# A two-graph attention network on one core: the edges' load, the masks' order, one buffer layout and the third border are changed

## The reference, cut to what matters

```python
e     = leaky_relu(s_src[src] + s_dst[dst], 0.2)      # one score per edge and head
emax  = segment_max(e, dst)
alpha = exp(e - emax[dst]) / segment_sum(exp(e - emax[dst]), dst)
out   = segment_sum(alpha[:, :, None] * h[src], dst) + bias
...
x = layernorm(x + gnn0(x, edges)); x = layernorm(x + gnn1(x, edges, types))
```

## Time and profile before

| | us |
|---|---|
| median of three runs | 1907.76 (1905.82 to 1907.84) |
| profiled execution, its own time | 1906.95 |
| its span, first to last instruction | 1905.1 |
| PE busy | 1777.2 (93%) |
| DVE busy | 1549.3 (81%) |
| ACT busy | 727.1 (38%) |

### The profile page before, as it was taken

How to read it: one execution, slowest core, us unless ns; L and a number is a source line. 1 busy time by engine, 2 the same in 40 slices (tenths; PEclk the granted TensorE clock), 3 DMA queues, 4 the chain that set the end, 5 groups by cost and what they waited for, 6 DMA issues and landing times.

```text
span 1905.1 us, 24263 instructions
## 1 busy us (share of the span) xinstructions
PE 1777.2 (93%) x8426; PEld 1337.9 (70%) x8427; DVE 1549.3 (81%) x2949; ACT 727.1 (38%) x1248; POOL 21.6 (1%) x40
## 2 busy tenths in 40 slices
PE   4889977699999899999999999998999999999997
PEld 3544545599754455555899999997899975555554
DVE  7898878899568555999999999996556648998996
ACT  4898976443124221111444444442311222332331
POOL 0000011010000000000000000000000000000000
PEclk8999998799999899999999999998999999999999
DMA  6200169351350326766412122121266467767764
GB/s 184 68 23 22 59 216 359 119 158 31 115 171 17 148 87 222 261 219 193 145 57 87 59 70 75 57 60 33 81 214 208 148 223 272 247 222 249 252 214 165
DMA packets 168068, 276.66 MB, mean 145 GB/s; under 512 B 11819, under 2 KB 132386, under 8 KB 164486
## 3 DMA queue, kind: packets, MB, share of 16 engines
q1 hardware_dynamic: 115942, 212.43, 34.4%
q10 hardware_dynamic: 48736, 48.48, 7.9%
q0 software_dynamic: 3264, 14.16, 2.1%
HBM read 219.31 MB, written 55.71 MB: 144 GB/s over the span
## 4 chain that ended last, share of the span: by engine, by line
PE 79%; DVE 12%; issue 3%; DMA 2%; ACT 2%; DVEq 1%; ACTq 0%; SPq 0%
PE ps L1406 26%; PE ps L1435 17%; PE ps L1359 12%; PE ps L1266 9%; PE ps L1064 3%; PE ps L1081 3%; PE ps L1169 2%; DVE work L1982 2%; PE ps L1198 2%; PE ps L1317 2%; DVE feat L2063 1%; DVE work L2394 1%; PE ps L1151 1%; DVE work L2388 1%; DVE feat L2359 1%
## 5 line engine op out<-in xcount | busy, mean ns | idle before, releaser
L1435 PE MATMUL ps<-work 128*128 128x384 f32 (+1 forms) x784 | 256.5, 486 | 2.0 <-DVE work L2149 2.0
L1359 PE MATMUL ps<-work 128*128 128x384 f32 (+1 forms) x720 | 237.9, 491 | 3.2 <-ACT work L1726 2.6
L1406 PE MATMUL ps<-counts,work 128*128 128x193 f32 x1440 | 239.3, 327 | 0.0
L1406 PEld LDWEIGHTS ps<-counts,work 128*128 128x128 f32 x1440 | 235.9, 190 | 0.3 <-DVE work L2394 0.3
L1820 ACT ACTIVATE work<-work,s 128x1280 f32<-128x1280 f32 x111 | 151.3, 1363 | 213.8 <-DVE work L2388 211.6
L1435 PEld LDWEIGHTS ps<-work 128*128 128x128 f32 x784 | 148.4, 189 | 107.1 <-DVE work L2149 2.6
L1359 PEld LDWEIGHTS ps<-work 128*128 128x128 f32 x720 | 136.9, 191 | 101.2 <-issue 16.3
L2394 DVE SCALAR_TENSOR_TENSOR work<-work,counts 128x1280 f32<-128x1280 f32 x112 | 166.3, 1485 | 2.0 <-SPq L569 2.0
L1406 PE MATMUL ps<-counts 128*128 128x193 f32 x960 | 160.9, 327 | 1.1 <-ACTq L569 1.1
L1982 DVE TENSOR_SCALAR work<-work,winoff 125x480 bf16<-125x480 f16 x480 | 158.4, 399 | 0.6 <-issue 0.5
L1406 PEld LDWEIGHTS ps<-counts 128*128 128x128 f32 x960 | 157.4, 190 | 1.7 <-ACTq L569 1.7
(11 more groups left out here) (295 smaller groups left out, 2597.8 us busy)
## 6 DMA issues: line engine op xcount, KB each, us to landing
work<-hs_d SPq DMA_DIRECT2D x75, 960.0 KB, 5.3
work<-nomask_d SPq DMA_DIRECT2D x70, 320.0 KB, 3.1
work<-pqrow_d SPq DMA_DIRECT2D x12, 1280.0 KB, 6.4
nomask_d<-work SPq DMA_DIRECT2D x40, 320.0 KB, 7.3
hx_d<-work ACTq DMA_DIRECT2D x60, 192.0 KB, 2.4
counts<-hx_d SPq DMA_DIRECT2D x120, 96.0 KB, 1.9
hs_d<-feat ACTq DMA_DIRECT2D x22, 480.0 KB, 3.6
counts<-pqrow_d SPq DMA_DIRECT2D x6, 1280.0 KB, 6.0
```

The costliest lines, as they stand in the source:

```text
L1359: last = mm(bank(n % 4 if i else n % 2, cols), xT[:, j, t * P:(t + 1) * P], wv[:, j, :], start=(j == 0), stop=(j == DT - 1))
L1406: last = mm(sums_at(c, t, u), xe_of(c)[i % RING][:, t * P:(t + 1) * P], hx[:, i % RING, 0:1 + c.width], start=(r == 0 and k == 0 and t % T ...
L1435: last = mm(bank(product_bank(g, i), width), a[:, at * P:(at + 1) * P], h_block(n, block_, width), start=(m == 0), stop=(m == STEPS_D - 1) ...
```

## The change

- SP waits for the edges before it issues `cols`, `wt_b`, `rhs` and `x`; ACT waits for the edges before it issues `wt_a`.
- The window bounds are computed for three chunks at once by six instructions; most of the edges' keys are made while PE turns the bounds; `bnd_ready` 3 lets ACT and PE read the table before `keys_ready`; ACT runs one small `Abs` early.
- Masks: the total mask of tile t+1 comes ahead of the type masks of tile t, and DVE alternates one mask and one search.
- `hx_a` moves from the masks' region to the front of `work`, with the `xe_a` buffers behind it. SP loads the features ahead of the last three masks' stores, DVE waits only until all masks are turned, and the first `weights` come ahead of the border.
- `keep_clock`: 24 transposes of the identity at the end of layer B, and 24, 24 and 16 around the first pieces of layer C.
- Before layer D ACT copies the turned tiles 0 and 1 each one `elu_exp` earlier.

```diff
-        hx_a = carve(work, (RING + 4) * NP, RING * H2C).rearrange("p (s c) -> p s c", s=RING)
+        hx_a = carve(work, 4 * NP, RING * H2C).rearrange("p (s c) -> p s c", s=RING)
-        xe_a = [carve(work, (4 + i) * NP, NP) for i in range(RING)]
+        xe_a = [carve(work, 4 * NP + RING * H2C + i * NP, NP) for i in range(RING)]
-        MASKS = [(TOTAL, 0)] + [(r if r < RELS else TOTAL, t if r < RELS else t + 1) for t in range(T) for r in range(RELS + 1)]
+        MASKS = [(TOTAL, 0)] + [m for t in range(T) for m in [*[(TOTAL, t + 1)] * (t + 1 < T), *((r, t) for r in range(RELS))]]
...
+            sp.wait_ge(e_in, 16 * 3)
             sp.dma_start(cols[:, :], t_in["cols"]).then_inc(cols_in, 16)
...
                     sp.dma_start(pqb_a[0], pqrow_d[0:2, :].partition_broadcast(P)).then_inc(s.pq_in[0].sem, 16)
+                    sp.wait_ge(v_done, len(WT_HALVES))
+                    for i in range(3):
+                        sp.wait_ge(*s.hx_out[i].at(16 * ring_share(2 * T, i, 3)))
+                    for k in range(RING):
+                        sp.dma_start(hx_a[:, k, 1:1 + HA], ga_d[k * P:(k + 1) * P, 0:HA]).then_inc(s.hx_in[k].sem, 16)
...
+            def keep_clock(n, at):
+                for _ in range(n):
+                    nc.tensor.transpose(ps[:, at:at + P // 2].bitcast(BF16), identb[:, :], identb[:, :])
...
+            pe.wait_ge(bnd_ready, 3)
+            extras = pe.value_load(tab[0:1, NW:NW + 1], min_val=0, max_val=MAXG)
             pe.wait_ge(keys_ready, 1)
-            extras = pe.value_load(tab[0:1, NW:NW + 1], min_val=0, max_val=MAXG)
...
                     b_attention(s)
+                    pe.wait_ge(o2_copied, 1)
+                    keep_clock(24, 2 * 512)
                     end_phase(pe, ph)
...
                     second_layer(0)
+                    keep_clock(24, 512)
                     second_layer(1)
+                    keep_clock(24, 512)
                     turn(0)
+                    keep_clock(16, 512)
...
-            act.wait_ge(s_chunkin, 32)
+            act.wait_ge(e_in, 16 * 3)
...
+            nc.scalar.activation(mm_[0:1, 0, 0:1], epsc[0:1, :], ACT.Abs)
+            act.wait_ge(bnd_ready, 3)
...
-                for e in range(3):
+                for e in range(2):
                     elu_exp(e)
-                fetch_turned(0)
-                elu_exp(3)
-                fetch_turned(1)
+                for e in range(2):
+                    fetch_turned(e)
+                    elu_exp(e + 2)
...
-            for a in range(3):
-                link(v.tensor_scalar(tmp_w, iota_w, cmin[:, a:a + 1], None, ALU.is_ge))
-                link(v.scalar_tensor_tensor(tmp_w, iota_w, cmax[:, a:a + 1], tmp_w, ALU.is_le, ALU.mult))
-                v.tensor_scalar(act_w[:, 0, a, :], tmp_w, cidm[:, a:a + 1], 1000.0, ALU.mult, ALU.add)
-                link(v.tensor_scalar(act_w[:, 1, a, :], tmp_w, cidp[:, a:a + 1], None, ALU.mult))
+            v.tensor_tensor(from_w, windows, by_chunk(cmin), ALU.is_ge)
+            link(v.tensor_tensor(upto_w, windows, by_chunk(cmax), ALU.is_le))
+            link(v.tensor_tensor(from_w, from_w, upto_w, ALU.mult))
+            link(v.tensor_tensor(act_w[:, 0, :, :], from_w, by_chunk(cidm), ALU.mult))
+            v.tensor_tensor(act_w[:, 1, :, :], from_w, by_chunk(cidp), ALU.mult)
+            link(v.tensor_scalar(act_w[:, 0, :, :], act_w[:, 0, :, :], 1000.0, None, ALU.add))
             v.nop().then_inc(bnd_ready, 1)
+            dve.wait_ge(e_in, 16 * 3)
+            ...   (five of the keys' instructions, two more behind bnd_ready 2, one behind bnd_ready 3)
             dve.wait_ge(bnd_turned, 1)
...
+                for t in range(T - 1):
+                    no_edges(4 * t + 1)
+                    dve.wait_ge(nm_copied, max(4 * t - 2, 1))
+                    if t == 0:
+                        dve.wait_ge(*s.s_in[0].at(16))
+                    search_a(t, 0)
+                    no_edges(4 * t + 2)
+                    search_a(t, 1)
+                    no_edges(4 * t + 3)
+                    if t == LAG:
+                        dve.wait_ge(*s.s_in[1].at(16))
+                    if t >= LAG:
+                        search_a(t - LAG, 2)
+                    no_edges(4 * t + 4)
+                    if t >= LAG:
+                        search_a(t - LAG, 3)
...
                 if c is A:
                     dve.wait_ge(v_turned, len(WT_HALVES))
+                    dve.wait_ge(nm_turned, 4 * T)
                     for i in range(2):
                         exponents(i, i, i, 0, 0, 16, 0, NP)
-                    for i in range(MASKS_OUT):
-                        dve.wait_ge(*nm_out_s[i].at(16 * ring_share(RELS * T, i, MASKS_OUT)))
                     v.memset(hx_a[:, :, 0:1], 1.0).then_inc(ones, 1)
+                    weights(0, 0, 0, c.rels[0], 0, NP)
```

More of the change, by code:

```diff
@@ L276, in gnn_program @@
         oh_hi = [take(WROW // 2, BF16) for _ in range(OH * WCH + 1)]
-        after_slots, space[0] = space[0], 16648 - 3272
+        after_slots, space[0] = space[0], 16648 - 3672
         src_i, dst_i, typ_i, win_i, tile_i = (take(NCH, I32) for _ in range(5))
@@ L281, in gnn_program @@
         cmin, cmax, cid, cidm, cidp = (take(4)[:, 0:3] for _ in range(5))
-        iota_w, tmp_w = take(NW), take(NW)
+        iota_w = take(NW)
+        from_w, upto_w = (take(3 * NW).rearrange("p (a w) -> p a w", a=3) for _ in range(2))
         act_w = take(6 * NW).rearrange("p (s a w) -> p s a w", s=2, a=3)
@@ L665, in _ @@
                 sp.wait_ge(*nm_out_s[i].at(16 * ring_share(RELS * T, i, MASKS_OUT)))
-            for i in range(3):
-                sp.wait_ge(*s.hx_out[i].at(16 * ring_share(2 * T, i, 3)))
-            for k in range(RING):
-                sp.dma_start(hx_a[:, k, 1:1 + HA], ga_d[k * P:(k + 1) * P, 0:HA]).then_inc(s.hx_in[k].sem, 16)
             for landed in total_out:
@@ L1531, in _ @@
             extras = act.value_load(tab[0:1, NW:NW + 1], min_val=0, max_val=MAXG)
+            act.wait_ge(keys_ready, 1)
             with act.If(extras < 1):
@@ L1934, in _ @@
             v.nop().then_inc(bnd_ready, 1)
+            v.scalar_tensor_tensor(keyf[0:EC, :], tile_i[0:EC, :], float(W), keyf[0:EC, :], ALU.mult, ALU.add)
+            v.scalar_tensor_tensor(lof[0:EC, :], tile_i[0:EC, :], -float(P), src_i[0:EC, :], ALU.mult, ALU.add)
             dve.wait_ge(bnd_turned, 2)
@@ L2068, in searches_a @@
                 no_edges(0)
-                for t in range(T + LAG - 1):
-                    masks = range(4 * t + 1, min(4 * t + 5, 4 * T))
-                    if t < T - 1:
-                        for n in masks:
-                            no_edges(n)
-                    if t < T:
-                        dve.wait_ge(nm_copied, 4 * t + 1)
-                        if t == 0:
-                            dve.wait_ge(*s.s_in[0].at(16))
-                        for h in (0, 1):
-                            search_a(t, h)
-                    if t == T - 1:
-                        rows_of_maxima(0)
-                        for n in masks:
-                            no_edges(n)
-                    if LAG <= t < T + LAG - 1:
-                        if t == LAG:
-                            dve.wait_ge(*s.s_in[1].at(16))
-                        for h in (2, 3):
-                            search_a(t - LAG, h)
+                for t in range(T - 1):
[14 more added lines that the diff above has]
+                        search_a(t - LAG, 3)
+                dve.wait_ge(nm_copied, 4 * T - 6)
+                for h in (0, 1):
+                    search_a(T - 1, h)
+                rows_of_maxima(0)
+                for r in range(RELS):
+                    no_edges(4 * T - RELS + r)
+                    if r < 2:
+                        search_a(T - 1 - LAG, 2 + r)
+                for t in range(T - LAG, T - 1):
+                    for h in (2, 3):
+                        search_a(t, h)
             def first_norm():
@@ L2414, in layer @@
                     return
-                if c is A:
-                    weights(0, 0, 0, c.rels[0], 0, NP)
-                elif c is C:
+                if c is C:
                     dve.wait_ge(bias_in, 16)
```

24 lines of the change are left out of this document (11 added, 13 removed).

## The result

| | before | after |
|---|---|---|
| median of the runs, us | 1907.76 (1905.82 to 1908.64, 5 runs) | 1899.33 (1893.85 to 1899.49, 5 runs) |
| profiled execution, us | 1906.95 | 1899.49 |
| its span, us | 1905.1 | 1897.7 |

The ratio is 0.9957 with a 95% interval of 0.9943 to 0.9971, 8.2 us less. The forecast was 14.6 less, 1893, with a range of 1886 to 1901: the sign and the range held, the size was 1.4 to 1.8 times too large.

What follows compares the result with a forecast made beforehand. PE, busy in 93% of the span, was taken as the bound. The terms -3.0 - 5.0 - 2.0 - 4.2 - 0.4 = -14.6 took the profiled 1906.95 us to 1892.4, median 1893; range 1886 to 1901.

Steps and rivals of the forecast that it cites:

- Start, -3.0: Kernel start to window 8: later loads delay the first statistics, but DVE's waits behind PE go; 42.2 in place of 45.19.
- Masks, -5.0: Mask 13 to the rows of maxima: alternating masks and searches removes DVE's idle time of 4.0 to 6.2 us; -5.0.
- the forecast stretch: Mask 13 to the rows of maxima, in the order by turns: 47.7 us, where the earlier trace had 52.7.
- the first search ahead of mask 2: First step of the masks: the search now ahead of mask 2 may cost one us, mostly regained.
- First border, -2.0: Rows of maxima to layer A's attention: PE starts about 18.5 us behind the rows in place of 20.55; -2.0.
- Third border, -4.2: Border to layer C: identity transposes fill PE's waits and keep its clock up; 653.1 in place of 657.28.
- the rival with 1900: Third border: identity transposes don't hold the clock and are paid at the lower one; +3.0 for -4.2, 1900; chance 0.12.
- Before layer D, -0.4: Border before layer D: only tile 1's copy by ACT comes one `elu_exp` sooner; -0.4, between 0 and -1.4.
- Whatever happens ahead of it simply shifts it: From 657 to 1313 PE is busy 651.4 of 655.7 us at clock 1.00, so nothing is to be had there.
- The slower rival: Masks: small pieces of work with waits drop PE to the lower clock; 1915 if in all twelve steps; chance 0.05.

Runs made afterwards that it cites:

- the last experiment: Mask 2 ahead of the first search in the first step, on the kernel with layer C's second weight piece earlier and identity turns between C and D: 1891.80 us, 0.9923.
- Four parts alone: Start, masks and searches by turns, first border, and third-border identity, each alone on the kernel before: 1900.96, 1903.53, 1905.17 and 1901.77 us.
- the turns alone: The kernel before with only the order of masks and searches changed, one mask and one search alternating: 1903.53 us, ratio 0.9985.
- the 60 turns: 60 identity transposes added ahead of the first mask, on the changed kernel with layer C's second weight piece one tile earlier: 1898.64 us, ratio 0.9962.

## Why the prediction was right in sign and too large

**Start, -3.0: right in size, for a wrong reason.** The step took the shift of the issues, 3.0 to 4.9 us, as the shift of the landings. The first statistics came 1.0 us earlier, not 1.7 later. From 10 to 20 us the queues moved 244 GB/s at a share of 1.04 in after and 247 in before: they are full, and what is issued later is only less deep in them. The fifth tile of `x` was issued 4.0 us later and landed 1.1 later (30.77 and 31.84). The bounds, the table load and the gap of DVE behind PE went as forecast. Window 8, the place of the forecast, was 4.7 us earlier and not 3.0, and the windows gave 1.2 of it back before the first mask, which no step had: that the first mask then came out 3.45 earlier, near the forecast, is luck.

**Masks, -5.0: the sum's most mis-sized term, -1.7 in the profiled execution, 1.3 on average of the traces, and 3 us by two comparisons of times, which hold other stages too.** The step named DVE as what is late next and let the stores "keep their queue". They keep it, but it is full: with three loads of weights on the way it runs at 410 GB/s, the five buffers come free late and ACT waits 3.8 to 7.8 us in the eight traces of this order with whole loads. With half the weights these waits are gone, and the forecast stretch appears to 0.4 us. How much of the shortfall is theirs is less sure, since the last experiment's trace had 3.8 us of them and took 47.9 us. The other part of the error was in the starting point: 52.7 us was taken from one trace, and the four other traces of the same order had 49.2, 49.2, 51.8 and 52.4. The one mishap that the step did price, the first search ahead of mask 2, was regained against before, as it said: mask 13 came 21.6 us behind the first mask in both. But there were 2.5 us more to be had there by one line.

**First border, -2.0: right at the border, and not kept.** -2.3 in the whole and -2.1 alone. The order of SP's issues behind `pqb_a` was right as well; the last store landed at 351.50, ahead of the end of DVE's `weights`. The sum then has nothing for layer A's attention, and that is where part of it goes. From its first product to its last it took 138.8 to 138.9 us in the four traces with the old border and 139.1 to 141.3 in the ten with the new one. In five of these PE waits 1.94 to 2.50 us for DVE some forty us into it, a low stretch of 3.4 us follows, and it takes 140.8 or more (after's +2.0 is one of them); in the other five the wait is 1.80 or less and it takes at most 139.6. From the rows of maxima to the end of layer A's attention that is 159.4 to 159.5 us with the old border; with the new one it is 157.2 to 157.6 where that low stretch is missing and 158.1 to 159.8 where it is there.

**Third border, -4.2: right in mechanism, small in size.** -5.0 with and without the other parts. The identity holds the clock at 1.00; the rival with 1900 is out. Most of the surplus is in the transposes: 24 of them, the turn and 16 more took 2.9 us from 636.58 to 639.48, where the sum had 3.5, so the third product started 0.1 us behind DVE's features and not 0.9.

**Before layer D, -0.4: right.** PE's next turn behind the first product came 13.8 us after the end of layer C's attention in all nine traces with this part, and 14.3 in the five without it: 0.5 us.

**"Whatever happens ahead of it simply shifts it": the step that failed.** It was drawn from the earlier trace rows, a stretch at 1.00 with PE busy for 99.3%. The 0.7% held a wait for a load that is issued by the progress of the same layer, behind loads that are not. It gave back 3.5 us in the profiled execution (1.8 as wait, 1.7 as low clock behind it: twelve products in 5.83 us, 4.14 in the traces without a drop). Issued a tile earlier it costs nothing, and the whole then gives 13.3 us. Four parts alone gave 5.1 + 2.9 + 1.5 + 4.8 = 14.3, each about 2 us uncertain. That is too wide to say whether the parts add: with the fifth part's 0.5, and the 0.8 us that the earlier load wins over before, 15.6 would be expected.

**Not settled.** The load of the second piece took 7.4 and 7.6 us from issue to PE's first product in the two traces of the changed kernel and 7.0 in that of the turns alone, but 5.8 to 6.2 in before and in five experiments, the turns with half the weights among them. So it was slow in all three traces that have the order by turns, whole loads of weights and the old place of the load, and in none of the others. Only where PE's wait was above 2 us did the low stretch follow. By what way the masks' order slows a load 350 us later wasn't found.

**The slower rival** (the masks at the lower clock, 1915) is out: from the first mask to the rows of maxima after had 22.5 us of 0.50, before 16.9. The first 12.2 of these run on from PE's wait of 5 us ahead of the first mask. The stretches among after's later masks, 10.2 us from 304.5 and 3.4 from 335.3, each came with a wait of PE, of 2.8 and 3.2 us. The Trainium skill ("TensorE: Matmul & The Clock Gate", section "A second HAM failure mode: psum-queue depth-cycling") would have had the clock swing for cycling banks between brief waits. In the same order with half the weights it stayed at 1.00 from 272.4 to 320.2, through 27 masks, which doesn't agree with the rule. But the drop at 320.2 came where PE had waited no longer than 1.1 us since 272, one at 306.1 in the last experiment behind waits of 1.2 and 0.8 us, and one at 305.1 with the 60 turns behind a wait of 1.4. In the other traces of this order the drops among the later masks came with waits of 2.1 to 3.7 us. So the rule is neither shown nor excluded here.

## What to carry to other kernels

A stretch in which the bounding engine is 99% busy is not a stretch that only shifts: look in its last per cent for waits on transfers, and ask of each what issues it and what stands ahead of it in the queue, before you count a gain ahead of it in full. A faster order of making things is worth no more than the stores behind it: compare the queues' busy share and GB/s with those of other stretches of the same trace. A gain read at the first instruction behind a border may be waited out at the next one: read it at the first instruction that waits for the engine which sets the pace. And a term read from one stretch of one trace should be read from a second execution too, where the clock falls in that stretch.

## What the runs showed of the hardware that was not expected

- Small transposes of a constant (62 ns each at the upper clock, 24 in 1.50 us) held the granted clock at 1.00 at two borders where PE's waits had been 1.0 to 4.1 us long, in all ten traces of the one and both of the other. 60 of them that started behind the wait, at the lower level, took 5.20 us, and the real work behind them came later.
- The upper clock was worth 0.5 us at a border where PE was at 0.50 for 10 us and waited for DVE and ACT between its pieces.
- Busy queues (share 1.04) hid most of a delay in the issue of the later loads, not of the first: the first tile of `x` went out at 9.70 in place of 4.85 and landed at 27.56 in place of 23.29, the fifth at 11.85 in place of 7.82 and landed at 31.84 in place of 30.77.
